# A macaron block (FFN, selective scan, FFN) on one core: weights transposed on the host, the first row begun while they land, the waits of an instruction named in another order

## The reference, cut to what matters

```python
x = x + 0.5 * ffn(layernorm(x), w_gate, w_up, w_down)      # weights: int32 in -127..127, times 1/127
x = x + attn(layernorm(x), W_z, W_params, conv_w, W_dt, b_dt, A_log, D, W_out)
x = x + 0.5 * ffn(layernorm(x), w_gate, w_up, w_down)
# ffn:  (silu(x @ wg.T) * (x @ wu.T)) @ wd.T, hidden size 768
# attn: dt = softplus(params[:, :64] @ W_dt.T + b_dt);  u = silu(causal conv of 4 taps over x)
#       A = -exp(A_log), 16 states n to each of 256 features
#       h[t] = exp(dt*A)[t-1] * h[t-1] + B~[t-1] * u[t-1];   y = sum over n of C[n] * h[n]
#       out = ((y + u * D) * silu(x @ W_z.T)) @ W_out.T
```

## Time and profile before

| what | us |
|---|---|
| median of 3 runs | 2757.11 |
| lowest and highest | 2753.33 and 2761.74 |
| the profiled execution, its own time | 2749.22 |
| its span in the trace | 2747.4 |
| DVE busy in the span | 2441.3 (89%) |
| POOL busy | 2160.6 (79%) |
| PE busy | 2123.0 (77%) |
| ACT busy | 2022.3 (74%) |
| first scan begins at | 156.95 |

### The profile page before, as it was taken

The page is one execution under the profiler, slowest core; times in us unless marked ns, Lnnn a source line. Parts: engine busy times, 40 slices in busy tenths (PEclk is TensorE's granted clock), DMA queues, the critical chain, the costliest instruction groups (busy, mean ns, idle before and its releaser), DMA issues.

```text
span 2747.4 us, 30026 instructions
## 1 busy us (share of the span) xinstructions
PE 2123.0 (77%) x9268; PEld 1156.8 (42%) x9268; DVE 2441.3 (89%) x2548; ACT 2022.3 (74%) x2885; POOL 2160.6 (79%) x1542
## 2 busy tenths in 40 slices
PE   4866688788878878787787878878787877877457
PEld 3433444444444444444444444444444444443234
DVE  3279998999999899999999998999999999999992
ACT  2568687787868778686887878687787868878553
POOL 1368888787878879787897978788798888879672
PEclk9977898888988888898999889898989988888678
DMA  1123333333333333333333333333333333333430
GB/s 60 40 89 134 120 119 108 120 112 130 109 122 124 108 118 116 128 116 115 131 114 117 113 127 114 114 127 106 116 123 131 115 117 130 105 112 116 138 112 19
DMA packets 112290, 308.06 MB, mean 112 GB/s; under 512 B 10913, under 2 KB 45826, under 8 KB 112130
## 3 DMA queue, kind: packets, MB, share of 16 engines
q1 hardware_dynamic: 112130, 306.15, 33.3%
HBM read 288.28 MB, written 17.83 MB: 111 GB/s over the span
## 4 chain that ended last, share of the span: by engine, by line
DVE 29%; PE 22%; issue 21%; POOL 17%; ACT 10%; DVEq 0%; SPq 0%; DMA 0%; POOLq 0%; ACTq 0%
DVE g_bank L960 12%; POOL acc L805 10%; DVE ring L991 10%; PE work L528 7%; PE work L539 5%; PE work L575 4%; DVE hid L919 3%; POOL hid_lo L777 2%; PE work L510 2%; DVE stats L906 2%; ACT ring L741 2%; ACT normed L619 2%; ACT L606 2%; POOL acc L796 1%; POOL rstd L768 1%
## 5 line engine op out<-in xcount | busy, mean ns | idle before, releaser
L805 POOL TENSOR_TENSOR acc<-acc,ring 128x1024 f32<-128x1024 f32 x512 | 1208.6, 2361 | 265.8 <-DVE ring L991 257.3
L960 DVE TENSOR_TENSOR_SCAN g_bank<-du_bank,ring 128x1024 f32<-128x1024 f32 x512 | 1173.4, 2292 | 35.1 <-ACT du_bank L730 4.7
L991 DVE SCALAR_TENSOR_TENSOR ring<-g_bank,inv_a,ring 128x1024 f32<-128x1024 f32 x512 | 653.9, 1277 | 8.5 <-POOL acc L805 1.1
L777 POOL TENSOR_TENSOR hid_lo<-hid,hid_hi 128x512 f16<-128x512 f32 x384 | 447.7, 1168 | 154.2 <-ACT hid_hi L688 153.8
L741 ACT ACTIVATE ring<-dt,a_coef 128x1024 f32<-128x1024 f32 x512 | 546.5, 1137 | 9.9 <-DVE g_bank L960 8.7
L539 PE MATMUL work<-wd_t,hid_hi 128*128 128x256 f16 x1536 | 372.2, 289 | 94.0 <-POOL hid_lo L777 80.2
L528 PE MATMUL work<-xt_hi,wg_t 128*128 128x512 f16 x768 | 323.7, 422 | 136.8 <-DVE hid L919 83.2
L528 PE MATMUL work<-xt_hi,wu_t 128*128 128x512 f16 x768 | 320.6, 417 | 119.0 <-DVE hid L919 66.2
L919 DVE SCALAR_TENSOR_TENSOR hid<-sil,work 128x512 f32<-128x512 f32 x384 | 259.2, 675 | 162.7 <-PE work L528 126.1
L539 PE MATMUL work<-wd_t,hid_lo 128*128 128x256 f16 x1536 | 370.7, 288 | 0.0
L653 ACT ACTIVATE sil<-work 128x512 f32<-128x512 f32 x384 | 219.4, 599 | 190.8 <-DVE hid L919 113.8
(11 more groups left out here) (98 smaller groups left out, 2899.7 us busy)
## 6 DMA issues: line engine op xcount, KB each, us to landing
ring<-c_rows SPq DMA_DIRECT2D x512, 512.0 KB, 3.6
x_in<-L_attn_x SPq DMA_DIRECT2D x32, 512.0 KB, 5.3
out<-x_fin SPq DMA_DIRECT2D x32, 512.0 KB, 5.3
c_rows<-params SPq DMA_DIRECT2D x32, 32.0 KB, 3.1
ring<-L_ffn_w_gate SPq DMA_DIRECT2D x1, 768.0 KB
ring<-L_ffn_w_up SPq DMA_DIRECT2D x1, 768.0 KB
ring<-L_ffn_w_down SPq DMA_DIRECT2D x1, 768.0 KB
ring<-L_attn_W_z SPq DMA_DIRECT2D x1, 256.0 KB
```

Source lines behind the costliest of these rows:

```text
L777: nc.gpsimd.tensor_tensor(hid_lo[:, m, :], hid[:, slot, :], hid_hi[:, m, :], ALU.subtract).then_inc(S["lo"], 1)
L805: nc.gpsimd.tensor_tensor(acc[bt % 2][:, h, :], acc[bt % 2][:, h, :], cg[:, slot, :], ALU.add).then_inc(S["summed"], 1)
L960: scan = nc.vector.tensor_tensor_scan(g_bank[:], du_bank[:], decay[:, a, :], 0.0, ALU.add, ALU.mult)
L991: nc.vector.scalar_tensor_tensor(cg[:, k, :], g_bank[:], inv_a[:, h, s:s + 1], spread[:, k_c, :], ALU.mult, ALU.mult).then_inc(S["weighted ...
```

## The change

Four things change, and the order of steps is not one of them.

1. The seven weight matrices are handed over transposed (`TURNED`), so the DMAs land them as PE needs them: `wp_t`, `wdt_t`, `wz_t` and `wo_t` directly, the three int32 ones in `ring`. Of the 50 turning matmuls 48 are gone with their copies L862; the last group (`inv_a_u`) now goes through `du_bank`.
2. The casts from int32 go to ACT, in row 0: gate and up just before its first `Te`, down before its second. `tap_diag` goes to ACT too, before the first `Te` of the second norm.
3. The DMAs stand in another order: `A_log`, the first half of x, gate, up, the second half of x, taps, down, and the rest. Each engine waits for what it needs at the step that needs it, through `hold`. DVE's constants no longer wait for any weight.
4. `wait` goes through `hold`, which leaves out a wait that the engine has already made for at least that count, and at eight places the calls are in another order.

The diff, cut to its core:

```diff
+        seen = {}
+
+        def hold(eng, s, n):
+
+            if seen.get((eng, s), 0) < n:
+                seen[eng, s] = n
+                eng.wait_ge(s, n)
...
-            eng.wait_ge({"ready": ready, "free": free}[what][s] if what in ("ready", "free") else S[s], n - less)
+            hold(eng, {"ready": ready, "free": free}[what][s] if what in ("ready", "free") else S[s], n - less)
...
+            sp.dma_start(a_coef[:], A_log.rearrange("(h p) n -> p h n", p=P)).then_inc(a_landed, 16)
+            load(0, 0)
+            sp.dma_start(st_g, w_gate.rearrange("(k p) m -> p k m", p=P)).then_inc(g_landed, 16)
+            sp.dma_start(st_u, w_up.rearrange("(k p) m -> p k m", p=P)).then_inc(u_landed, 16)
+            load(0, 1)
+            sp.dma_start(taps[:], conv_w.rearrange("(h p) o k -> p h (o k)", p=P)).then_inc(w_landed, 16)
+            sp.dma_start(st_d, w_down.rearrange("(m p) e -> p m e", p=P)).then_inc(d_landed, 16)
...
-                (st_z.rearrange("p (h e) -> p h e", h=EH), W_z.rearrange("(h p) e -> p h e", p=P)),
...
+                (wp_t[:, :, 0:R], W_params[:, 0:R].rearrange("(k p) m -> p k m", p=P)),
+                (wp_t[:, :, C_ROW:C_ROW + N], W_params[:, R + N:R + 2 * N].rearrange("(k p) m -> p k m", p=P)),
+                (wdt_t[0:R, :], W_dt),
                 (wdt_t[R:R + 1, :], b_dt.rearrange("(o e) -> o e", o=1)),
+                (wz_t[:], W_z.rearrange("(k p) e -> p k e", p=P)),
+                (wo_t[:], W_out.rearrange("(k p) e -> p k e", p=P)),
...
-            pe.wait_ge(w_set, 3)
-            n = 0
...
-            for w in (st_g, st_u):
-                for k in range(EH):
-                    for m0 in (0, 4):
-                        turn_group([w[:, m * E + k * P:m * E + (k + 1) * P] for m in range(m0, min(m0 + 4, HM))])
...
-            turn_group([inv_a_u[:, h, :] for h in range(EH)])
...
+            pe.wait_ge(s_tiny, 1)
             pe.matmul(g_bank[0:1, 0:EH * N], ones[:], tiny[:].rearrange("p h n -> p (h n)"), start=True,
                       stop=True).then_inc(s_flag, 1)
-            pe.wait_ge(w_kept, groups)
-            pe.wait_ge(s_flag, 3)
+            pe.wait_ge(s_inv, 1)
+            for h in range(EH):
+                last = pe.transpose(du_bank[0:PROWS, h * P:(h + 1) * P], inv_a_u[:, h, :], ident[:])
+            last.then_inc(s_turned, 1)
...
+                    hold(pe, s_cast, 1 if kind == "ga" else 2)
...
+                    hold(pe, s_cast, 3)
...
+                    hold(pe, w_landed, LANDED)
+                    hold(pe, s_pads, 1)
...
-            act.wait_ge(w_landed, 16 * 11)
+            act.wait_ge(a_landed, 16)
             nc.scalar.activation(a_coef[:], a_coef[:], ACT.Exp).then_inc(s_exp, 1)
-            act.wait_ge(w_kept, groups)
-            act.wait_ge(s_set, 1)
...
+                    wait(act, "rstd", ("lr",) + ev[1:])
                     wait(act, "ready", K.was[ev])
-                    wait(act, "rstd", ("lr",) + ev[1:])
...
+                    if (f, bt, c) == (1, 0, 0):
+                        for dst, src, landed in ((wg_t, st_g, g_landed), (wu_t, st_u, u_landed)):
+                            act.wait_ge(landed, 16)
+                            nc.scalar.activation(dst[:], src, ACT.Copy).then_inc(s_cast, 1)
+                    elif (f, bt, c) == (1, 0, 1):
+                        act.wait_ge(d_landed, 16)
+                        nc.scalar.activation(wd_t[:], st_d, ACT.Copy).then_inc(s_cast, 1)
+                    elif (f, bt, c) == (2, 0, 0):
+                        act.wait_ge(w_landed, LANDED)
+                        for k in range(EH * KW):
+                            last = nc.scalar.activation(tap_diag[:, k // KW, k % KW, :], ident[:], ACT.Identity,
+                                                        scale=taps[:, k // KW, k % KW:k % KW + 1])
+                        last.then_inc(s_cast, 1)
...
+                    hold(act, s_kept, 1)
+                    wait(act, "scanned", ("scan", bt, N - 1, h - 1) if h else ("scan", bt - 1, N - 1, EH - 1))
+
                     wait(act, "du", ("d", bt, h))
-
-                    wait(act, "scanned", ("scan", bt, N - 1, h - 1) if h else ("scan", bt - 1, N - 1, EH - 1))
...
-            pool.wait_ge(w_kept, groups)
-            pool.wait_ge(s_set, 1)
+            pool.wait_ge(s_pads, 1)
...
+                    wait(pool, "weighted", ev)
                     if s == 0:
                         wait(pool, "acc_begun", ("ai", bt, h, NC - 1))
-                    wait(pool, "weighted", ev)
...
-            dve.wait_ge(w_landed, 16 * 11)
-            for w in (st_g, st_u, st_d):
-                then(nc.vector.tensor_copy(w, w.bitcast(I32)))
-
-            for t in (wp_t[:], inv_a_u, xt[:, :, 0:KW - 1], u[0][:, :, 0:1], u[1][:, :, 0:1]):
-                then(nc.vector.memset(t, 0.0))
+            for t in (wp_t[:, :, R:C_ROW], xt[:, :, 0:KW - 1], u[0][:, :, 0:1], u[1][:, :, 0:1]):
+                nc.vector.memset(t, 0.0)
+            nc.vector.memset(minus_half[:], -0.5)
+            nc.vector.memset(eps[:], EPS)
+            nc.vector.memset(params[R:R + 1, :], 1.0).then_inc(s_pads, 1)
...
-            for h in range(EH):
-                for k in range(KW):
-                    then(nc.vector.tensor_scalar(tap_diag[:, h, k, :], ident[:], taps[:, h, k:k + 1], None, ALU.mult))
...
+            nc.vector.tensor_scalar(tiny[:], a_coef[:], A_MIN, None, ALU.is_lt).then_inc(s_tiny, 1)
+            dve.wait_ge(s_tiny, 1)
+            nc.vector.tensor_scalar(a_coef[:], a_coef[:], -1.0, None, ALU.mult).then_inc(s_set, 1)
+            dve.wait_ge(s_set, 1)
...
-            def keep(copies):
-                nonlocal n
-                dve.wait_ge(w_turned, n + 1)
-                for dst, src in copies(work[n % BANKS]):
-                    last = nc.vector.tensor_copy(dst, src)
-                last.then_inc(w_kept, 1)
-                n += 1
...
+            nc.vector.tensor_scalar(neg_ident[:], ident[:], -1.0 / XS, None, ALU.mult).then_inc(s_inv, 1)
             dve.wait_ge(s_flag, 1)
-            nc.vector.tensor_reduce(flag_f[:], g_bank[0:1, 0:EH * N], AX_X, ALU.add).then_inc(s_flag, 1)
+            nc.vector.tensor_reduce(flag_f, g_bank[0:1, 0:EH * N], AX_X, ALU.add).then_inc(s_flag, 1)
             dve.wait_ge(s_flag, 2)
-            nc.vector.tensor_copy(flag[:], flag_f[:]).then_inc(s_flag, 1)
+            nc.vector.tensor_copy(flag[:], flag_f).then_inc(s_flag, 1)
+            dve.wait_ge(s_turned, 1)
+            nc.vector.tensor_copy(wdt_t[C_ROW:C_ROW + N, :], du_bank[C_ROW:C_ROW + N, 0:E]).then_inc(s_kept, 1)
             dve.wait_ge(s_flag, 3)
-            dve.wait_ge(w_kept, groups)
             n_tiny = dve.value_load(flag[0:1, 0:1])
...
+                        wait(dve, "ready", job)
                         wait(dve, "free", ("ga",) + ev[1:])
-                        wait(dve, "ready", job)
...
+                        wait(dve, "weighted", earlier(ev, 1))
+                        wait(dve, "decay", ("ex",) + ev[1:])
                         if s == 0:
                             wait(dve, "du_in", ("db", bt, h))
-                        wait(dve, "decay", ("ex",) + ev[1:])
-
-                        wait(dve, "weighted", earlier(ev, 1))
...
-        a = np.ascontiguousarray(inputs[name])
+        a = np.ascontiguousarray(inputs[name].T if name in TURNED else inputs[name])
...
```

95 lines of the change are left out of this document (31 added, 64 removed).

## The result

| what | before | after |
|---|---|---|
| median, us | 2755.61 | 2714.98 |
| lowest and highest | 2753.33 and 2761.74 | 2712.83 and 2717.73 |
| the profiled execution, its own time | 2749.22 | 2717.73 |
| its span | 2747.4 | 2715.9 |
| first statistics begin | 36.92 | 12.62 |

After over before is 0.9846, with a 95% interval of 0.9826 to 0.9865. The change made the kernel 40.6 us faster between the medians; 44.9 had been forecast. The two profiled executions lie only 31.5 us apart, because the one of before lies 6.4 us under its median and the one of after 2.7 above.

What follows compares the result with a forecast made beforehand. DVE was taken to set the pace. The first scan coming 23.2 us earlier plus 21.7 us from the waits made 44.9 us off the span of 2747.4, so 2702.5, or 2712 us as median; range 2697 to 2735.

Steps and rivals of the forecast that it cites:

- The prologue: Start of the kernel, up to the first statistics: row 0 begins 25.5 us earlier (21 to 26), at 11.4 us.
- The second rival: Branch before the first statistics: its code waits for the weights, row 0 begins at about 17.5, 2718 us; chance 0.08.
- What ACT takes over: Row 0 before the first scan: casts on ACT cost 0.3 us, the eight `tap_diag` 2.0 us.
- The gaps: DVE's scans directly behind a `cm`: holding the wait for `weighted` themselves saves 285 x 0.069 = 19.7 us.
- not all of it stays: Scans followed by a stall for PE before L919: 32 x 0.069 = 2.2 us taken off the gaps' gain.
- `sh` and the semaphore instructions: `sh` holding its PE wait itself saves 3.4 us over 49 waits; removed semaphore instructions on ACT and PE save 0.8.
- The slower case: PE: one more whole matmul group per row at the lower clock, 79 us more, 2791 us; chance 0.04.

Runs made afterwards that it cites:

- held-weights run: The kernel after, with SP holding back the DMAs of `w_gate` and all behind it until the first statistics are done: 2715.06 us.
- `tap_diag` on POOL: The kernel after, with the eight `tap_diag` written by POOL in its idle time in row 0 and not by ACT: 2714.76 us.
- the head alone: The kernel after with the old wait order at all six places and no waits left out: 2737.82 us, ratio 0.9929 to before.
- Without the collision: The kernel after with the product of `ai` kept in its PSUM bank: 2670.78 us; with the scan's two waits also in old order: 2676.88 us.
- The order of waits alone: The kernel before with the wait calls in the new order at the same six places, nothing else: 2737.51 us, ratio 0.9919.
- the leaving out: The kernel before with only `hold` put in, leaving out waits an engine has already made: 2751.64 us, ratio 0.9979.

## Why the prediction was right, and where it was not

The time, 2714.98, lies 3 us above the 2712 predicted and inside the range. Step by step:

**The prologue** (forecast 25.5 us earlier, found 24.3). Two errors of opposite sign. `A_log` was taken to land at 3.8 us, by a 32 KB row; its exponential began at 2.78. The branch was taken as 3.9 us with 0.6 added for the load; its wait alone is 6.38, which is 2.8 more than before. The mechanism was named, and its term was mis-sized: 2.8 and not 0.6. The held-weights run shows the 3.04 without load, so the load costs 3.3 us. The second rival, code that waits for the last weight (row 0 at 17.5), is out.

**What ACT takes over** (forecast 2.3). A cast takes 1.47 us and not 1.7, and the first `xt_hi` followed at once. `tap_diag` takes 0.30 us each, 2.43 in all, and not 2.0; `tap_diag` on POOL shows it on the path. The estimate by the Trainium skill ("VectorE: DVE Perf Modes", the TRN2 errata), 2.3, was nearer than mine. Altogether the first scan came 21.5 us earlier and not 23.2, and the head by itself gave 19.4 (15 to 24).

**The gaps** (forecast 19.7 less 2.2). The gap behind a `cm` fell from 0.104 to 0.035 us on the mean, in 285 cases, and idle time before the scans by 19.8 us. With nothing but the scan's two waits put back it was 34.6 again: who holds the wait is the cause, as said. The step that failed is the next one, "not all of it stays", which took off 2.2 us for stalls and nothing for anything else. In steady rows nearly nothing of it stays. With the scan's waits put back, a row takes the same 160.4 us on the mean: the gain is spent on L933 colliding with POOL, which takes as much as the gaps and the shorter waits for PE gave together. Without the collision it is spent on waits for PE, and a row takes 157.0 either way. That DVE's busy time would be unchanged was wrong for the same reason; L933 was not looked at, since it is 4% of DVE's time, although its mean of 1409 ns, about twice the 675 of the other instruction of the same shape and operation, `hid`, was there to be seen.

**Why the sum was nevertheless right.** The order of waits alone did give 19.7 us. In the traces they are not in the typical row. They are in the first and last rows, and in that before and the head alone have some rows of 162.4 to 163.1 us among those of 160.4 to 161.4, which the kernels with the new order do not have (before also has two short ones of 158.3). With the head alone the thirteen rows in the middle take 161.25 us on the mean, with the whole change 160.4; that is 10.5 of the 19.6 us between these two from first to last scan. So a figure worked out from one mechanism was met by another, and that they agree is luck. What makes the long rows is not settled. The order at the scan alone does not: the kernel with only the scan's waits put back has no row over 161.3 us. The length of the last two L950 differs among them, but that it drives the row is not shown.

**`sh` and the semaphore instructions** (3.4 and 0.8). The first was worked out from 49 waits, and with the 29 under "issue" it is 78. Behind PE's matmul `hid` began after 0.094 us before the change and after 0.037 with it, so 78 x 0.057 = 4.4 us are gone from these waits. In time it was not measured apart. An estimate: the head alone and the kernel with the scan's waits put back differ by the other five places and the leaving out, 9.1 us, and less the 5.5 of the leaving out that is some 3.6. The second came to 5.5 us alone on before and to 0.5 where rows repeat; the larger figure belongs to the long rows again.

**The slower case** was not seen: PEclk is 0.91 and 0.88 in the stretches where it was 0.88 and 0.87.

**What stays open**: what bounds a row at 157.0 us. DVE is idle for some 9 us of it, PE and POOL for over 20. The waits go round, DVE for PE's `up` and PE for DVE's `hid`, inside one FFN chunk, so the loop through them with the scans that the fixed order puts in between is the likely one. No run here changed it.

## What to carry to other kernels

Before a gain in small gaps is counted, ask what in a steady row repeats and what it waits for: here the steady rows gave back what one engine gained (160.4 us and 157.0 with either order of the scan's waits), and the gain showed only in the first and last rows. A group whose mean duration differs from another of the same shape and operation, or whose shortest and longest lie far apart, may be waiting inside its instruction, as L933 was; that waiting counts as busy, so no idle column shows it. Put a branch so that the likely side follows it, and never where DMAs are at their busiest.

## What the runs showed of the hardware that I had not expected

- A `scalar_tensor_tensor` of 128x512 with all operands in SBUF takes 0.75 us alone and up to 2.96 beside a POOL `tensor_tensor` of 2.36 us, ending 0.55 us after it; with one operand in PSUM it takes 0.746 to 0.751 us in all 64 cases. Where DVE was first by 0.10 us, POOL's took 2.87.
- A branch to code that stands elsewhere, with the load of its flag, costs 3.0 us with idle queues and 6.4 under DMA load; falling through costs 0.25.
- Behind its producer on DVE an instruction starts after 0.035 us when it holds the wait itself, and after 0.104 when a semaphore instruction ahead of it does; behind a matmul of PE it is 0.037 and 0.094.
- The first small DMA has landed 2.8 us after the start of the span at the latest, with the x and weight loads queued behind it.
- Eight `tap_diag` of 128x128 take 2.43 us on ACT and 4.68 us on POOL.
